# Attention kernel: a V tile moved by one head group, output tiles and normalisation spread over other steps

## What is computed

```
q  = layer_norm(x, ln1) @ wq + bq         k = ctx @ wk + bk      v = ctx @ wv + bv
s  = q k^T / sqrt(32), masked so that row i sees columns 0..i
o  = softmax(s) @ v
x1 = x + o @ wo + bo
y  = x1 + gelu(layer_norm(x1, ln2) @ w1 + b1) @ w2 + b2
```

## Time and profile before

| | |
|---|---|
| median of three runs | 2957.35 us |
| profiled execution | 2956.78 us |
| its span, first to last instruction | 2955.1 us |
| mean granted TensorE clock | 0.989 |
| PE busy | 2786.7 us, 94% |
| VectorE (DVE) busy | 2033.4 us, 69% |
| ScalarE (ACT) busy | 1654.5 us, 56% |
| GpSimd (POOL) busy | 355.2 us, 12% |
| batches of stage A, start to start | 93.2 us |

### The profile page before, as it was taken

How to read it: one execution, slowest core, us unless ns; L and a number is a source line. 1 busy time by engine, 2 the same in 40 slices (tenths; PEclk the granted TensorE clock), 3 DMA queues, 4 the chain that set the end, 5 groups by cost and what they waited for, 6 DMA issues and landing times. The chain is left out here.

```text
span 2955.1 us, 65575 instructions
## 1 busy us (share of the span) xinstructions
PE 2786.7 (94%) x22056; PEld 2510.5 (85%) x22056; DVE 2033.4 (69%) x4884; ACT 1654.5 (56%) x4014; POOL 355.2 (12%) x364
## 2 busy tenths in 40 slices
PE   6999999999999999999984999999999899999999
PEld 4777777787777877777764999999999899999999
DVE  4766676667776677666756877877787766665566
ACT  3655666566655666566644565556556544444444
POOL 1211222112221122212210000000000000000000
PEclk9999999999999999999997999999999999999999
DMA  6666666667665676666634344334435343333442
GB/s 139 112 116 108 111 110 121 114 106 110 118 121 99 114 110 122 115 100 121 98 64 150 136 170 184 135 142 185 170 123 219 135 156 142 142 142 122 155 156 93
DMA packets 151738, 383.03 MB, mean 130 GB/s; under 512 B 12160, under 2 KB 16256, under 8 KB 143488
## 3 DMA queue, kind: packets, MB, share of 16 engines
q1 hardware_dynamic: 151680, 382.28, 52.8%
HBM read 172.51 MB, written 109.05 MB: 95 GB/s over the span
## 5 line engine op out<-in xcount | busy, mean ns | idle before, releaser
L711 ACT ACTIVATE sm<-sm,mins 128x128 f32<-128x128 f32 (+3 forms) x1024 | 571.6, 559 | 570.5 <-DVE mins L574 567.9
L574 DVE CUSTOM_DVE_ANT_0 sm<-bank_s,mask 128x128 f32<-128x128 f32 (+3 forms) x1024 | 480.6, 488 | 418.5 <-PE bank_s L425 416.2
L437 PE MATMUL bank_t<-ident,sm 128*128 128x128 f32 x2560 | 418.8, 278 | 73.8 <-DVE pT L520 37.4
L437 PEld LDWEIGHTS bank_t<-ident,sm 128*128 128x128 f32 x2560 | 299.6, 141 | 178.3 <-issue 58.3
L425 PE MATMUL bank_s<-stack 96*128 96x128 f32 (+3 forms) x1024 | 353.0, 386 | 8.4 <-DMA stack<-st_lo 7.9
L520 DVE COPY pT<-bank_t 128x384 f32<-128x384 f32 (+1 forms) x576 | 326.8, 567 | 1.3 <-PE bank_t L437 1.3
L1092 PE MATMUL bank_x<-b_hi,w_hi 128*128 128x256 f32 x1024 | 296.8, 290 | 26.9 <-ACT g L1515 21.6
L1092 PE MATMUL bank_x<-w_hi,a_hi 128*128 128x256 f32 x1024 | 291.2, 284 | 4.0 <-DVE a_lo L1212 4.0
L1093 PE MATMUL bank_x<-b_lo,w_hi 128*128 128x256 f32 x1024 | 291.1, 284 | 0.0
L1094 PE MATMUL bank_x<-b_hi,w_lo 128*128 128x256 f32 x1024 | 291.1, 284 | 0.0
L1094 PE MATMUL bank_x<-w_hi,a_lo 128*128 128x256 f32 x1024 | 290.9, 284 | 0.0
(11 more groups left out here) (178 smaller groups left out, 7389.4 us busy)
## 6 DMA issues: line engine op xcount, KB each, us to landing
stack<-st_hi SPq DMA_DIRECT2D x256, 256.0 KB, 6.1
xt<-in_x SPq DMA_DIRECT2D x32, 1024.0 KB, 5.1
stack<-st_lo SPq DMA_DIRECT2D x128, 256.0 KB, 7.3
xr<-x_scratch SPq DMA_DIRECT2D x32, 1024.0 KB, 5.6
b_scratch<-b_hi SPq DMA_DIRECT2D x16, 1792.0 KB, 10.0
b_scratch<-b_lo SPq DMA_DIRECT2D x16, 1792.0 KB, 13.7
b_hi<-b_scratch SPq DMA_DIRECT2D x16, 1792.0 KB, 7.5
b_lo<-b_scratch SPq DMA_DIRECT2D x16, 1792.0 KB, 11.2
```

The lines of the kernel that those rows point to most:

```text
L437: mm = pe.transpose(bank_t[n % 2][:, P * c:P * c + P], sm[:, n % SLOTS_S, P * c:P * c + P], ident[:])
L574: op = V.tensor_tensor_reduce(sm[:, n % SLOTS_S, off:off + w], bank_s[n % BANKS_S][:, off:off + w], mask[:, 512 - w:512], 1.0, 0.0, ALU.ad ...
L711: op = A.activation(row, row, ACT.Exp, bias=mins[:, g % 2, c:c + 1], scale=-1.0, accum_out=sums[:, g % 2, c:c + 1])
```

## The change

Four things are edited, all in stage A: the output tiles O1 and O2 are spread over two steps each, and O3 comes a step later; V0b leaves steps 10 and 11 of group 1 for steps 7 and 8 of group 2; X0 to X3 move to steps 9, 10, 11 and 11; the statistics, the normalisation and one copy (`O_HIGH_LATE`, for group 1 alone) move to later steps. The waits that name V0b's place follow: the first use of V0b in group 2, and the wait of POOL before it converts the next context.

```
-[("Q2", {0: 6, 1: 6}), ("K2", {2: 6, 3: 6}), ("R", {4: 4}), ("O1", {5: 12}), ("O2", {7: 12}), ("O3", {8: 6, 9: 6}), ("V0b", {10: 12, 11: 12})],
-[("Q3", {0: 6, 1: 6}), ("K3", {2: 6, 3: 6}), ("R", {4: 4}), ("V1b", {5: 12, 6: 12}), ("X0", {7: 4}), ("X1", {8: 4}), ("X2", {9: 4}), ("X3", {10: 4})],
+[("Q2", {0: 6, 1: 6}), ("K2", {2: 6, 3: 6}), ("R", {4: 4}), ("O1", {5: 6, 6: 6}), ("O2", {7: 6, 8: 6}), ("O3", {9: 6, 10: 6})],
+[("Q3", {0: 6, 1: 6}), ("K3", {2: 6, 3: 6}), ("R", {4: 4}), ("V1b", {5: 12, 6: 12}), ("V0b", {7: 12, 8: 12}), ("X0", {9: 4}), ("X1", {10: 4}), ("X2", {11: 4}), ("X3", {11: 4})],
...
-R_AT, PV1_AT, PV0_AT, O_PROD_AT, O_HIGH_AT, O_HIGH_LATE = 4, 5, 9, 6, 7, 10
+R_AT, PV1_AT, PV0_AT, O_PROD_AT, O_HIGH_AT, O_HIGH_LATE = 4, 5, 9, 6, 7, 11
-STATS_AT, NORMALISE_AT = (1, 3, 4, 4), (5, 6, 6, 7)
+STATS_AT, NORMALISE_AT = (3, 4, 5, 6), (7, 8, 9, 10)
...
-at = {"V0a": -1, "V1a": 0, "V0b": 1, "V1b": 2}[name]
+at = {"V0a": -1, "V1a": 0, "V0b": 2, "V1b": 2}[name]
...
-pool.wait_ge(dense, it.done("V1b", 2))
+pool.wait_ge(dense, it.done("V0b", 2))
```

## The result

The changed kernel takes 2964.45 us (median of 11 runs, 2959.38 to 2966.58), the kernel before 2957.35 (11 runs, 2953.73 to 2960.13). The ratio is 1.0024, 95% interval 1.0016 to 1.0031: +7.1 us. The profiled execution took 2961.76 us, 5.0 more than that of before; its mean granted clock is 0.983, against 0.989.

A forecast was written before the change was run, and what follows sets the result against it. Group 1 was taken as bound by PE, group 2's end by VectorE and ScalarE work for normalised x. Middle batches -8.4, first +0.4, last -1.0: -9.0 from 2956.78, given as 2948.0 us, range 2934.5 to 2957.5.

The forecast's parts named there:

- Group 1: Bound by PE; V0b's 24 matmuls leave and step 11 has nothing dense: -2.8 us a batch, to about 24.5 us.
- Group 2, steps 5 to 8: V0b's halves in steps 7 and 8 nearly fill PE's 1.22 us hole; step 9's scores come at 860.82 instead of 860.26.
- Group 2, steps 9 to 11: X3 waits 1.3 us for normalise 3, Q0 1.1 us for x_low; Q0 starts 2.2 us later a batch.
- The collision with POOL: Rival, chance 0.09: normalise 2 and 3 wait beside POOL's conversions, up to 1.28 us a batch longer; 2966 us.
- The load of x: x lands 7.2 us into group 2, first statistics read it at 7.3; cost 0. Rival, x late: 2984 us, chance 0.05.
- Margin 0.1 us: Time between x landing and VectorE reaching its first statistics in step 3 of group 2; lateness up to 0.8 us costs nothing.
- The bound of 10.5 us in every batch: Other bound for the load of x: the longest landing in every batch, costing about 3 us each.
- The granted clock is 1.00 in all three, so nothing here is a matter of clock: Read from three stretches of batch 8 before the change; the clock was given no cost.
- The last batch: No X work there: -2.8 us, but two light steps in group 2 go from 2.2 to 4.0: -1.0.
- -8.4: Sum over 14 middle batches at -0.6 us each, from -2.8 in group 1 and +2.2 in group 2.

The follow-up runs named there:

- e3: The kernel before with V0b moved to steps 7 and 8 of group 2, X0 to X3 to steps 8, 9, 10 and 10: 2959.33 us, ratio 1.0009.
- e4: The kernel before with only X0 to X3, statistics and normalisation at their new places; V0b and output tiles unmoved: 3008.68 us, ratio 1.0180.
- e10: The changed kernel with sixteen transposes in both waits, POOL's o_low and conversions held until normalise 3 is done: 2968.73 us, ratio 1.0041 to the kernel before.
- e2: The changed kernel with eight unused transposes before X3's wait and eight before Q0's in batches 0 to 14: 2952.96 us, ratio 0.9987 to the kernel before.
- e7: The changed kernel with eight unused transposes before Q0's wait alone: 2954.43 us, ratio 0.9991 to the kernel before.
- e8: The changed kernel with eight unused transposes before X3's wait alone: 2954.53 us, ratio 0.9986 to the kernel before.
- e5: The changed kernel with statistics and normalisation earlier, X0 to X3 in steps 7, 9, 9, 10, X0 ahead of V0b: 2957.4 us, ratio 0.9996 to the kernel before.

## Why the prediction was wrong, step by step

- **Group 1.** Right. Forecast -2.8 us and 24.5 us in all; measured -2.86 and 24.43, step 11 without idle time (0.56 us). The forecast gave all of it to V0b; e3, which moves V0b alone, gets 2.0.
- **Group 2, steps 5 to 8.** Right in its main point: V0b fills the hole of step 8, and e4 shows that it costs nothing at all there. One term was too small: normalise 1 was put at 0.45 and took 1.22 beside o_low.
- **Group 2, steps 9 to 11.** The chain was the right one: normalise 3, X3, x_high, x_low 3, Q0, with two new idle times put down to L544 and L552. Forecast: Q0 11.4 us after step 7. Measured 11.72, which puts Q0 2.5 us later than before instead of 2.2, and 11.38 in e10, where no normalise is disturbed. That 11.38 is so close to 11.4 is in part luck, for the single waits were off both ways: X3's wait was 0.9 instead of 1.3, Q0's 0.93 instead of 1.1, and step 10 had 0.46 that I had at 0.1.
- **The collision with POOL.** I gave it a chance of 0.09, as a rival, since "nothing says these fell beside a conversion". It was there in every middle batch. By e10 it costs 0.35 us a batch, about 5 us in all; I had priced it at 1.28 a batch, so that the rival's 2966 lies near the measured time is luck. The Trainium skill, "GPSIMD Engine Reference", Specifications, names the case: SBUF interfaces that GpSimd shares with VectorE, and contention with VectorE instructions that use two ports or have two SBUF inputs. These traces agree (SBUF holds the tiles, PSUM the results of TensorE): normalise went from 0.54 to as much as 1.52 us beside POOL and POOL's cast from 0.61 to 0.80; x_low, with one input in PSUM, stayed at 0.68.
- **The load of x.** Margin 0.1 us forecast, and it was about that. After the kernel's first load, for which both kernels wait, VectorE waited eight times for x, 7.8 us in all, most of it covered: outside batch 1 no group 2 is over 25.38 us. Batch 1 was not: x landed 8.2 us after its issue, and VectorE stood for 2.96 us; its group 2 is 1.1 us longer. Cost 1 us, forecast 0. The bound of 10.5 us in every batch was misread: that is the first batch's load alone, all others of the kernel before landed within 5.3.
- **The step that failed: "The granted clock is 1.00 in all three, so nothing here is a matter of clock".** That reads the clock of a schedule that the change takes apart. I forecast two new pauses of 1.3 and 1.1 us close together, put the clock's cost at nothing, and did not ask what it would do after them. It fell in six of fourteen middle batches, at 1.6 us each, some 9 us in all. e2, e7 and e8 show the cause for the middle batches. The Trainium skill, "TensorE: Matmul & The Clock Gate", A second HAM failure mode: psum-queue depth-cycling, tells of a kernel in which short idle times of TensorE between groups of matmuls, frequent enough, brought the low clock back again and again. These traces agree, with idle times of 0.46, 0.90 and 0.93 us. I trusted a row of before for a stretch that would no longer be the same.
- **The last batch.** Forecast -1.0; it came out at +3.1, with 13.7 us at 0.50 in one piece. Groups 0 to 2 gave -1.3, so the schedule is about as forecast, and the +4.3 of group 3 is the low clock. After e4 this can't simply be put down to the change, and why the clock falls there stays open.

Without the clock, the schedule is worth 14 x -0.3 = -4 us in the middle batches; I said -8.4. Of the 4 us between, the collision is the whole. From there to the measured +7.1, the low clock of the middle batches gives some 9 and x about 1; the rest lies in the first and last batch and in parts that the change doesn't touch, which differ from execution to execution. The 0.9987 of e2 is -3.8 us, but its trace has a last batch 3.0 us longer and a first one 1.3 shorter than before, so that it meets the -4 so closely is in part luck.

## What to carry to other kernels

A list of due times moves waits as well as work: before work is moved into a hole, ask what made the hole (here VectorE's list for x), for moving that later can cost as much as the filling brings. Where a change leaves several idle times of TensorE close together, the granted clock of before says nothing on the one after; a few matmuls that nothing uses, in a pause that is there anyway, tell on one run whether the clock is the price. And before VectorE's work is shifted to stand beside GpSimd's, look how the same instruction fared beside GpSimd in a trace: here the normalise, from SBUF to SBUF, was held, and masks, pT copies and x_low, which read PSUM, were not.

## What the runs showed of the hardware that was not expected

- Two idle times of 0.9 us, 1.2 us apart from end to start, with 0.46 us idle before them, were followed by 3.4 us at 0.50 of the clock in six of fourteen batches of the same schedule; with either one filled, in none. The low stretch cost 1.6 us. The kernel before idled longer (2.7 us, spread over 6.7) and kept its clock.
- A normalise of 128x512 float32 in SBUF took 0.54 us alone and 0.64 to 1.52 when it started beside one of POOL's subtractions of two SBUF tiles. It then ended 0.28 to 0.29 us after that subtraction did, in 45 of 45 cases of the changed kernel and 29 of 29 in e5, whatever was left of the subtraction. In e5 a subtraction that began 0.19 us into a normalise took 1.49 instead of 1.28; a cast next to a held normalise went from 0.61 to 0.80.
- The same load of x (1 MB) landed 4.9 to 5.3 us after its issue from batch 1 on in the kernel before, where the next transfer was issued 7.7 us behind it (batch 8), and 4.9 to 8.2 in the changed kernel, where stack copies follow after 3.4. The 10.5 us of the earlier trace rows is the load of the first batch alone, in both.
